# Moving the source-list load ahead of the second pair in a two-layer graph network on one Trainium2 core

## The reference, cut to what matters

```python
edge_index = jnp.stack([src, dst])
x = _layernorm(x + _L0_gnn_ref(x, edge_index, edge_attr_4, edge_attr_16, ...))
x = _layernorm(x + _L1_gnn_ref(x, node_vec1, edge_attr_16, edge_attr_4, src, dst, ...))
# layer 0: xs_e = xs[src]; xv_e = xv[src]; products with edge_feat and the weights,
#          messages * sigmoid(edge_scalars @ W_rad.T + b_rad); segment_sum over dst
# layer 1: e0 = f0[edge_src]; e1 = f1[edge_src]; products with w = silu(...) @ Wfc2 and sh;
#          segment means over dst, then node products
```

## Time and profile before

| what | value |
|---|---|
| runs of the kernel before | 5918.03, 5922.7, 5962.53 us; median 5922.7 us |
| span of the profiled execution | 5900.5 us |
| median of the runs over that span | 22.2 us |
| layer 0's gathers | 66.1 to 2860.0 us |
| layer 1's gathers | 2993.4 to 5801.4 us |

### The profile page before, as it was taken

How to read it: one execution, slowest core, us unless ns; L and a number is a source line. 1 busy time by engine, 2 the same in 40 slices (tenths; PEclk the granted TensorE clock), 3 DMA queues, 4 the chain that set the end, 5 groups by cost and what they waited for, 6 DMA issues and landing times.

```text
span 5900.5 us, 82997 instructions
## 1 busy us (share of the span) xinstructions
PE 3955.8 (67%) x16478; PEld 2613.9 (44%) x16479; DVE 3891.0 (66%) x12732; ACT 3383.0 (57%) x10841; POOL 3146.9 (53%) x3275
## 2 busy tenths in 40 slices
PE   5555555555565565565667777778777777777776
PEld 3444444444444444454544343434434334344345
DVE  4666666666666666666656666667666666666666
ACT  3556655655655565665555565555555555555554
POOL 4555555555555555555345555555555555555551
PEclk7555555555555555555688888888888888888888
DMA  7555555555555555555332222222222222222222
GB/s 232 140 142 143 141 145 139 141 144 139 141 145 140 138 146 139 139 145 142 90 81 75 74 75 74 78 73 77 75 74 75 73 72 75 73 76 77 74 76 53
DMA packets 325631, 641.98 MB, mean 109 GB/s; under 512 B 143598, under 2 KB 175131, under 8 KB 325499
## 3 DMA queue, kind: packets, MB, share of 16 engines
q0 software_dynamic: 181584, 557.89, 34.8%
q1 hardware_dynamic: 144016, 83.72, 5.4%
HBM read 620.47 MB, written 20.88 MB: 109 GB/s over the span
## 4 chain that ended last, share of the span: by engine, by line
DVE 34%; another core or an unknown queue 23%; PE 22%; issue 12%; DVEq 4%; ACT 3%; DMA 1%; POOL 0%; SPq 0%; ACTq 0%
PE ps L907 15%; DVE work L625 10%; DVE onehot L660 7%; DVE work L609 5%; ACT work L433 3%; PE ps L900 3%; DVE work L612 2%; PE ps L892 2%; DVEq L676 2%; DVE work L648 2%; DVE dstf L704 1%; DVEq L721 1%; DVE work L655 1%; DVE acc L668 1%
## 5 line engine op out<-in xcount | busy, mean ns | idle before, releaser
L361 POOL DMA_INDIRECT arena<-table,srcs x1616 | 1541.1, 954 | 1292.1 <-issue 486.4
L361 POOL DMA_INDIRECT work<-table,srcs x1616 | 1560.7, 966 | 1249.9 <-issue 435.9
L433 ACT ACTIVATE work<-arena,dst_sh 128x96 f32<-128x96 f32 (+1 forms) x4848 | 1416.3, 378 | 569.9 <-DVE arena L632 496.1
L907 PE MATMUL ps<-work,onehot 128*128 128x384 f32 x3616 | 1493.6, 564 | 176.7 <-DVE work L655 114.8
L433 ACT ACTIVATE work<-work,dst_sh 128x96 f32<-128x96 f32 (+1 forms) x4848 | 1499.1, 398 | 21.0 <-issue 11.0
L883 PE MATMUL ps<-wrad,escal 17*128 17x160 f32 x3232 | 561.7, 495 | 1195.2 <-DVE arena L632 1119.4
L907 PEld LDWEIGHTS ps<-work,onehot 128*128 128x128 f32 x3616 | 754.5, 218 | 842.8 <-issue 534.0
L907 PE MATMUL ps<-arena,onehot 128*128 128x161 f32 x3616 | 1077.2, 478 | 10.3 <-issue 7.5
L883 PEld LDWEIGHTS ps<-wrad,escal 17*128 17x128 f32 x3232 | 406.0, 309 | 1349.2 <-DVE arena L632 866.0
L907 PEld LDWEIGHTS ps<-arena,onehot 128*128 128x128 f32 x3616 | 921.4, 319 | 138.9 <-issue 128.0
L517 ACT ACTIVATE hid<-ps 128x256 f32<-128x256 f32 x404 | 152.2, 377 | 1197.6 <-remote 867.7
(11 more groups left out here) (122 smaller groups left out, 2090.2 us busy)
## 6 DMA issues: line engine op xcount, KB each, us to landing
escal<-in_escal SPq DMA_DIRECT2D x404, 98.0 KB
arena<-table,srcs POOLq DMA_INDIRECT x1616
work<-table,srcs POOLq DMA_INDIRECT x1616
table<-work SPq DMA_DIRECT2D x49, 224.0 KB, 3.2
dst_sh<-in_dst_sh SPq DMA_DIRECT2D x404, 20.0 KB
table<-work SPq DMA_DIRECT2D x7, 784.0 KB, 4.0
acc<-in_xd SPq DMA_DIRECT2D x1, 3920.0 KB
arena<-in_xd SPq DMA_DIRECT2D x7, 560.0 KB, 4.2
```

The source lines that it names most:

```text
L361: pool.indirect_dma_start(out=rows[:, j, t, :], out_offset=None, in_=table, in_offset=bass.IndirectOffsetOnAxis(ap=srcs[:, b, j, t:t + 1], ...
L433: last = nc.scalar.activation(u[:, t, to:to + c1 - c0], r[:, t, c0:c1], ACT.Copy, scale=dst_sh[:, j, at:at + 1].bitcast(f32))
L907: last = mm(bank(to)[:, 0:(MSG0, MSG1)[l]], onehot[:, b, t, :], m[:, j % 2, t, :], start=t == 0, stop=t == TPS - 1)
```

## The change

The list load, with its four waits for gathers, moves from behind both pairs of a round to behind the first pair (c = 0). What it loads, into which buffer and on which semaphore stay the same.

```diff
                         sp.sem_inc(s_sp, 1)
                         sp.wait_ge(s_add[l], s + PAIR + 2)
                         load_dst_sh(l, s + SLOTS, c)
-                    if lists:
-                        for j in range(SLOTS):
-                            sp.wait_ge(s_rows[l][j], (r + 1) * 16 * TPS)
-                            if j < SLOTS - 1:
-                                sp.sem_inc(s_sp, 1)
-                        load_src(l, (r + 2) * SLOTS, b)
+                        if lists and c == 0:
+                            for j in range(SLOTS):
+                                sp.wait_ge(s_rows[l][j], (r + 1) * 16 * TPS)
+                                if j < SLOTS - 1:
+                                    sp.sem_inc(s_sp, 1)
+                            load_src(l, (r + 2) * SLOTS, b)
```

## The result

The changed kernel takes 5724.73 us (median of 4 runs, 5697.97 to 5735.73), the kernel before 5934.42 us (4 runs, 5918.03 to 5962.53) on the same chip: a ratio of 0.9645 with an interval of 0.9602 to 0.9687. Forecast were 5773 us, 2.5% faster; measured are 3.5%.

The account below looks back on a forecast made before the run. A loop of waits bounds the kernel: POOL's gather issuing plus two stops per round. Rounds falling to 27.0 us save 70 + 80 = 150 us, giving 5773 us; own range 5690 to 5860, overall 5400 to 5950 us.

Parts of the forecast that it names:

- The bound: In each round, POOL's issuing of 16 gathers (20.0 us) plus two stops (3.3 and 4.2 us) makes 27.5 us.
- 102 such waits: DVE's waits for "remote" in layer 0, cited for adds told late, 2.5 us after POOL's last gather.
- The list wait goes to nothing: POOL's wait before slot 0, 745.6 us over both layers, falls to near 0; the list is at least 9 us early.
- The turn of two slots: On POOL: add, 2.0 us, eight gathers in 9.8 us, 1.65 us, next add; 13.5 us, so 27.0 us a round.
- Its stops: POOL's stops for DVE or ACT: twice a round, about 3.7 us each, some 200 in a layer.
- Runs of eight gathers: Two-slot runs on POOL in both layers, 27.0 us a round; gains 70 + 80 = 150 us; chance 0.46.
- (B): Rival: runs of three slots become the rule, 19.2 us each, 25.6 us a round; 430 us gained, 5493 us; chance 0.20.
- Span to median: Whole kernel: medians lie 22.2 us above the profiled span, so a span of 5750.5 us becomes 5772.7 us.
- (D): Rival, slower: each run of eight is followed by 2.5 us, a turn 14.3 us; 170 us lost, 6093 us; chance 0.09.
- (A): Rival: all 687 us gained, POOL's stop for DVE staying 4.2 us once a round; 5236 us; chance 0.11.
- (C): Rival: no difference, 5923 us, as POOL's stop for DVE grows by just what the list wait was; chance 0.14.

## Why the prediction was right, and where it was not

**The bound: right.** POOL's issuing plus its stops was the whole round, and "while POOL issues gathers without a pause, what PE has finished is told late" stands for most of the late adds (in the trace of before, 193 of the 257 that had waited over 1 us start behind a run's end): cutting the runs gave 5180 us, and on chips where the news isn't late there are hardly any stops. Its "102 such waits" are all of layer 0's waits for "remote", not only those that end so.

**The list wait goes to nothing: right**, from 745.6 us to none. The load is issued 13.2 us ahead of its use in the median (forecast: about 10), `escal` and `dst_sh` cost nothing that shows, and a gather stays at 0.946 us.

**The turn of two slots, 13.5 us: right**, 13.1 us in layer 0 and 13.6 us in layer 1. Its stops came as forecast too, some 200 in a layer of about 3.7 us: there were 180 and 191 of over 1.2 us, and what a round has above 20.0 us gives them about 3.4 and 4.1 us each.

**"Runs of eight gathers", 27.0 us a round in both layers: wrong.** That step took one kind of turn for all. Runs of eight are 67 and 69 of the turns, and runs of twelve, the rival (B), 64 and 59. In layer 0 they took the 19.3 us that (B) gave them, 25.8 us a round, so the mean of the two came to 26.1 us and 158 us were gained in place of 70. In layer 1 a run of twelve took 21.9 us, 29.2 us a round, and ate up the rest: 13 us in place of 80. The sum, 171 us against 150, was near by luck of opposite errors. Why layer 1's long runs end in a 7 us stop and layer 0's don't is partly seen (the silu and the weighting stand behind the same news on ACT), but that they are dearer because of the change isn't shown: the kernel with the change in layer 0 alone has as long stops for ACT in layer 1.

**Span to median, 22.2 us: misread.** For the changed kernel the execution with a span of 5733.9 us took 5735.73 us, 1.8 us more. So the 22.2 us were mostly the difference between one execution and the median, and not what a launch adds. By the spans the change is worth 166.6 us, by the medians 209.7 us. The 43 us between them are why layer 1's share stays uncertain.

**(D), (A) and (C)** did not come on this chip. (C), no difference, is the whole truth on others: 0.9999, for another reason than it gave: where PE's news is prompt, the list is in time in either place (2.7 us of list waits in a whole layer of the old order).

## What to carry to other kernels

Before you price a wait that you take away, ask what else happens in that pause. Here it let other engines' news through, and of 687 us only some 170 to 210 stayed gained. Price every kind of turn that the new order can fall into, with its share, and not the commonest one alone. And measure on more than one chip before you keep a version: with the pause of 1.1 us per slot the changed kernel takes 12% less than the kernel before where that one takes 5916 us, and the kernel before with the same pause loses 15.6% where it takes 4393 us.

## What the hardware showed that was not expected

The same program takes 5934, 5916 or 6014 us on some chips and 4390 to 4394 us on others, with the gathers' issue at 946 ns on all and nearly the same granted clock in layer 0 (0.54 and 0.56). In layer 1 the clocks differ, 0.83 against 0.98, as the rounds do. Within one set of runs the kernel before kept to its kind, but no chip was used in two sets, so it may be the chip or something else that holds for a whole set of runs. What differs is whether PE's news comes through while POOL issues indirect DMAs back to back. It depends on the length of the gap after each four of them (at 0.7 us 859 us of stops are left, at 1.1 us 88 us) and not on the bytes they move (80 in place of 150 GB/s, 26.0 us a round in place of 26.1). What in the chip does this, and why only on some, is open. Whether the longer pause helps the changed kernel as much on a second chip where the kernel before takes some 5900 us wasn't measured either.
